# Weight transfers of 4 MB with 32 KB rows, in a ring of four buffers and a fifth beside it

## What is computed

```
x = _L0_conv_ref(x, style, 2, 13)       # 13x13 Gaussian means and deviations of x and style: (x-mean_x)/std_x*std_s+mean_s
x = _L1_conv_ref(x, weights of L1)      # attention over patches and windows, below
x = _L2_conv_ref(x, w1, b1, w2, b2)     # two 3x3 convolutions, relu between, + x
x = _L3_conv_ref(x, weights of L3)      # as L1, other weights

# L1 and L3: PD = 1024, WD = 16384, 4 windows (of 32x32), 16 patches (of 8x8) in each, 8 heads
fl = _ln(xf, pn_g, pn_b)                                     # 64 patches x 1024
pf = _merge(_attn(fl, Wqk_p) @ _heads(fl @ Wv_p) + _dwconv(...)) @ Wout_p
ww = _attn(_ln(pl, pln_g, pln_b), Wqk_w, WDH)                # 4 x 4 per head, from the pooled image
wv = _heads(_ln(xw, wn_g, wn_b) @ Wv_w)                      # 4 x 16384 @ 16384 x 1024
wf = _merge(nds @ wv + _dwconv(wv, ...)) @ Wout_w            # 4 x 1024 @ 1024 x 16384
out = diag_scaled * pf + wf + x
```

## Time and profile before

| | us |
|---|---|
| median of 3 runs | 762.57 |
| lowest, highest | 761.68, 762.76 |
| span of the profiled execution, first to last instruction | 760.3 |
| TensorE busy in it | 499.3 (66%) |
| VectorE busy | 92.3 (12%) |
| DMA queue 1, share of the 16 engines' time | 99.1% |
| bytes moved | 320.82 MB |

### The profile page before, as it was taken

How to read it: one execution, slowest core, us unless ns; L and a number is a source line. 1 busy time by engine, 2 the same in 40 slices (tenths; PEclk the granted TensorE clock), 3 DMA queues, 4 the chain that set the end, 5 groups by cost and what they waited for, 6 DMA issues and landing times.

```text
span 760.3 us, 7405 instructions
## 1 busy us (share of the span) xinstructions
PE 499.3 (66%) x3076; PEld 143.4 (19%) x3076; DVE 92.3 (12%) x254; ACT 38.0 (5%) x79; POOL 8.8 (1%) x19
## 2 busy tenths in 40 slices
PE   6599675556556656565677979565665576666565
PEld 5234210000002211121122433000000121111121
DVE  3754400000001000000006071000000100000000
ACT  2111100000000000000001010000000000000000
POOL 2100000000000000000001000000000000000000
PEclk9589898786878777878897989978677877768789
DMA  9999999999999999999999999999999999999996
GB/s 367 427 391 431 427 428 428 429 428 428 428 428 429 428 428 428 428 428 429 428 428 427 424 428 427 431 428 428 428 428 428 428 428 428 428 430 428 429 428 280
DMA packets 22856, 320.82 MB, mean 422 GB/s; under 512 B 2569, under 2 KB 2689, under 8 KB 3257
## 3 DMA queue, kind: packets, MB, share of 16 engines
q1 hardware_dynamic: 22464, 320.04, 99.1%
q10 hardware_dynamic: 377, 0.56, 0.2%
HBM read 320.10 MB, written 0.49 MB: 422 GB/s over the span
## 4 chain that ended last, share of the span: by engine, by line
DMA 72%; PE 20%; DVE 6%; issue 1%; ACT 1%; SPq 0%; DVEq 0%; ACTq 0%
DMA ring<-stream 71%; PE bank L341 4%; PE bank L452 3%; PE bank L429 3%; PE bank L407 2%; DVE conv_p L772 2%; PE bank L350 2%; PE bank L259 1%; DMA cst<-const 1%; PE bank L358 1%; PE bank L476 1%; PE bank L270 0%; DVE l_sq L644 0%; PE bank L312 0%; PE bank L474 0%
## 5 line engine op out<-in xcount | busy, mean ns | idle before, releaser
L452 PE MATMUL bank<-ring,wf_t 128*32 128x512 f32 x1024 | 169.3, 797 | 99.1 <-DMA ring<-stream 93.7
L429 PE MATMUL bank<-ring,stage 128*4 128x512 f32 x1024 | 162.3, 773 | 107.5 <-DMA ring<-stream 107.5
L452 PEld LDWEIGHTS bank<-ring,wf_t 128*32 128x32 f32 x1024 | 32.7, 131 | 215.3 <-DMA ring<-stream 147.8
L429 PEld LDWEIGHTS bank<-ring,stage 128*4 128x4 f32 x1024 | 24.7, 94 | 243.3 <-DMA ring<-stream 163.6
L259 PE MATMUL bank<-cst,area 128*128 128x128 f32 (+1 forms) x234 | 38.5, 318 | 15.3 <-ACT area L579 11.6
L259 PEld LDWEIGHTS bank<-cst,area 128*128 128x128 f32 (+1 forms) x234 | 32.9, 219 | 43.9 <-ACT area L579 33.8
L847 DVE TENSOR_TENSOR image<-bank,image 128x32 f32 (+1 forms) x30 | 5.1, 194 | 278.3 <-PE bank L259 278.3
L341 PE MATMUL bank<-ring,area 128*64 128x512 f32 x128 | 33.7, 692 | 1.7 <-DVE area L728 1.7
L821 DVE COPY wv_t<-bank 128x32 f32<-128x32 f32 x2 | 0.4, 192 | 275.4 <-PE bank L259 275.4
L579 ACT COPY area<-bank 128x512 f32<-128x512 f32 x15 | 8.8, 586 | 282.3 <-PE bank L452 282.3
L407 PE MATMUL bank<-ring,area 128*64 128x512 f32 x64 | 18.0, 727 | 0.0
(11 more groups left out here) (193 smaller groups left out, 196.4 us busy)
## 6 DMA issues: line engine op xcount, KB each, us to landing
ring<-stream SPq DMA_DIRECT2D x151, 2048.0 KB, 35.5
ring<-stream SPq DMA_DIRECT2D x2, 1024.0 KB, 35.8
l_in<-images SPq DMA_DIRECT2D x1, 512.0 KB, 4.4
cst<-const SPq DMA_DIRECT2D x1, 461.0 KB, 5.6
area<-window_gains ACTq DMA_DIRECT2D x1, 256.0 KB, 4.6
windows_last<-area SPq DMA_DIRECT2D x1, 256.0 KB, 2.0
out<-l_in ACTq DMA_DIRECT2D x2, 112.0 KB
area<-small ACTq DMA_DIRECT2D x1, 52.0 KB
```

Of the source, the lines that this page charges most:

```text
L429: m = mm(bank[0][32 * j:32 * j + 4, :], stage[:, k // 8, at:at + 4], w[:, j], start=False, stop=False)
L452: m = mm(bank[6 + g][32 * j:32 * j + 32, :], wf_t[:, h, :], w[:, j], start=(h == 0 and onto is None), stop=(h == GROUP - 1))
```

## The change

- Every transfer of weights is four slots (`QUARTER`), 128 rows of 32 KB, except the last four slots: the last eight go as 4, 2, 1 and 1 slots (`LAST_CUTS`).
- `ring` stays 128 KB of a partition, now four places of four slots. A fifth place, `extra`, 32 KB, holds the first and the sixth four-slot piece of each layer. The six pieces ("quarters") are Wqk_p, Wv_p, Wqk_w and Wout_p.
- Wv_w and Wout_w are laid out on the host in blocks of eight slots ("halves"), 128 rows of 64 KB. A transfer takes one half of each row: 32 KB out of every 64 KB. In `quarters` rows are 32 KB and stand one after another.
- The work areas of the first stage lie in the ring's last place, so that the fifth piece waits for `image_turned`; `out_rows` lies in `extra`.
- TensorE waits once for four slots where it waited once for two. SyncE's waits follow: a place is filled again when its four slots have been used. In the second layer the pieces 1 and 2 wait for the first half of the first layer's last turn, the pieces 3 and 4 for all of it, and piece 0 for nothing of its own.
- The semaphore per buffer becomes one per piece and place: `quarter_landed`, `part_landed`, `last_landed`. A parameter makes the memory set aside for descriptors that software writes smaller.

The matmuls, their operands' shapes and their order stay as they are, and so does the work of ScalarE, VectorE and GpSimd.

```
-        ring = sb("ring", P, RING, PAIR * SLOT)
+        ring = sb("ring", P, TURN * SLOT)
+        extra = sb("extra", P, QUARTER * SLOT)
...
+        front = ring[:, 3 * QUARTER * SLOT:]
+        l0_in = front[:, 0:C * IMG].rearrange("p (c x) -> p c x", c=C)
...
+        out_rows = extra[0:IMG, 0:2 * BANK]
...
+            at = None if j in (0, N_QUARTERS - 1) else (j - 1) * QUARTER * SLOT
+            return extra[:, :] if at is None else ring[:, at:at + QUARTER * SLOT]
...
-            for k in range(RING):
-                sp.dma_start(ring[:, k, :], stream[k]).then_inc(ring_landed[k], 16)
-            def slots_free(t, k):
-                sp.wait_ge(slots_used, t * (RING * PAIR) + ((k + 1) * PAIR - RING * PAIR))
-
-            with sp.Fori(1, N_BUFFERS // RING - 1) as t:
-                for k in range(RING):
-                    slots_free(t, k)
-                    sp.dma_start(ring[:, k, :], stream[t * RING + k]).then_inc(ring_landed[k], 16)
...
+            def load_quarter(L, j):
+                sp.dma_start(quarter_of(j), quarters[L * N_QUARTERS + j]).then_inc(quarter_landed[j], 16)
+
+            def load_part(L, t, c):
+                lo = c % 2 * QUARTER * SLOT
+                sp.dma_start(ring[:, c * QUARTER * SLOT:(c + 1) * QUARTER * SLOT],
+                             halves[t * 2 + (L * N_HALVES + c // 2)][:, lo:lo + QUARTER * SLOT]).then_inc(part_landed[c], 16)
+
+            for L in range(2):
+                load_quarter(L, 0)
+                for j in range(1, N_QUARTERS - 1):
+                    if L:
+                        sp.wait_ge(slots_used, used(L, -HALF if j < 3 else 0))
+                    elif j == N_QUARTERS - 2:
+                        sp.wait_ge(image_turned, 1)
+                    load_quarter(L, j)
+                sp.wait_ge(slots_used, used(L, QUARTER))
+                load_quarter(L, N_QUARTERS - 1)
+
+                for c in range(4):
+                    sp.wait_ge(slots_used, used(L, (c + 2) * QUARTER))
+                    load_part(L, 0, c)
+                with sp.Fori(1, 2 * TURNS - L) as t:
+                    for c in range(4):
+                        sp.wait_ge(slots_used, t * TURN + (used(L, S_VW) + (c + 1) * QUARTER - TURN))
+                        load_part(L, t, c)
...
+            for n, landed in enumerate(last_landed):
+                lo, hi = LAST_CUTS[n], LAST_CUTS[n + 1]
+                sp.wait_ge(slots_used, used(1, S_VW) + t * TURN - HALF + hi)
+                sp.dma_start(ring[:, (HALF + lo) * SLOT:(HALF + hi) * SLOT],
+                             halves[2 * N_HALVES - 1][:, lo * SLOT:hi * SLOT]).then_inc(landed, 16)
```

More of the change, by code:

```diff
@@ L102, in constants, with build @@
     return c
-def build(nc, images, const, window_gains, small, l2w, stream, out, windows_last):
+def build(nc, images, const, window_gains, small, l2w, quarters, halves, out, windows_last):
     with ExitStack() as ctx:
@@ new lines, in _ @@
+            t = 2 * TURNS - 1
+            for c in range(2):
+                sp.wait_ge(slots_used, used(1, S_VW) + t * TURN + (c + 1) * QUARTER - TURN)
+                load_part(1, t, c)
+            for n, landed in enumerate(last_landed):
[3 more added lines that the diff above has]
+                             halves[2 * N_HALVES - 1][:, lo * SLOT:hi * SLOT]).then_inc(landed, 16)
@@ L259, in turn, with quarter_there, part_there @@
                 return mm(dst, src, ident[0:rows, 0:rows], start=True, stop=True)
[L261 to L264, removed]
+            def quarter_there(L, s):
+                if s % QUARTER == 0:
+                    pe.wait_ge(quarter_landed[s // QUARTER], 16 * (L + 1))
+            def part_there(L, t, c):
+                pe.wait_ge(part_landed[c], t * 16 + 16 * (L * 2 * TURNS + 1))
             pe.wait_ge(const_landed, 16)
@@ L421, in _ @@
                 with pe.Fori(0, TURNS) as i:
[L422 to L423 removed]
+                    for k in range(TURN):
+                        if k % HALF == 0:
                             pe.wait_ge(staged, i * 2 + (2 * TURNS * L + k // 8 + 1))
[L425 to L426 removed]
+                        if k % QUARTER == 0:
+                            part_there(L, i, k // QUARTER)
+                        w = slot_of(S_VW + k).rearrange("p (j n) -> p j n", j=4)
                         for j in range(4):
@@ L445, in group @@
                     for h in range(GROUP):
[L446 to L450, removed]
+                        if onto is None and h % QUARTER == 0:
+                            part_there(L, i + TURNS, g * 2 + h // QUARTER)
+                        elif onto is not None and h in LAST_CUTS:
+                            pe.wait_ge(last_landed[LAST_CUTS.index(h)], 16)
+                        w = slot_of(S_OUTW + g * GROUP + h).rearrange("p (j n) -> p j n", j=4)
                         for j in range(4):
@@ L888, in dram @@
         return nc.dram_tensor(name, a.shape, mybir.dt.from_np(a.dtype), kind="ExternalInput").ap()
-    gains, smalls, pieces = [], [], []
+    gains, smalls, first, rest = [], [], [], []
     for n in ("L1_conv", "L3_conv"):
@@ L895 @@
         smalls += [v[k].reshape(P, 9).T for k in ("conv_p_w", "conv_w_w")]
-        pieces += [in_tiles(arr(f"{n}_{k}"), PAIR * SLOT // arr(f"{n}_{k}").shape[1]) for k in ("Wqk_p", "Wv_p", "Wqk_w", "Wout_p", "Wv_w")]
+        first += [in_tiles(arr(f"{n}_{k}"), QUARTER * SLOT // arr(f"{n}_{k}").shape[1]) for k in ("Wqk_p", "Wv_p", "Wqk_w", "Wout_p")]
+        rest += [in_tiles(arr(f"{n}_Wv_w"), HALF * SLOT // PD)]
         out_w = arr(f"{n}_Wout_w")
-        pieces += [in_tiles(out_w[:, at:at + SLOT], PAIR) for at in range(0, WD, SLOT)]
-    stream = dram("stream", np.concatenate(pieces))
+        rest += [in_tiles(out_w[:, at:at + SLOT], HALF) for at in range(0, WD, SLOT)]
+    quarters, halves = dram("quarters", np.concatenate(first)), dram("halves", np.concatenate(rest))
     l2w = np.concatenate([arr(f"L2_conv_{k}").transpose(1, 2, 3, 0).reshape(C, 9 * C) for k in ("w1", "w2")]
```

65 lines of the change are left out of this document (32 added, 33 removed).

## The result

| | kernel before | changed kernel |
|---|---|---|
| median, us | 762.18 (761.68 to 762.76, 4 runs) | 755.18 (754.87 to 755.32, 4 runs) |
| ratio | | 0.9906, 95% interval 0.9894 to 0.9918 |
| span of the profiled execution, us | 760.3 | 753.0 |
| packets | 22856 | 12056 |

The change makes the kernel 7.0 us faster, 0.94%. The forecast was 757.6 us with a range of 754.3 to 763.0: the sign and the range held. The forecast gain was 4.9 us and the measured one is 7.0; the rest of the 2.4 is that the kernel before has a median of 762.57 us ahead of the prediction and of 762.18 here. Two more comparisons of the same two kernels, on other chips, gave 0.9902 and 0.9907.

A forecast was written before the change was run, and what follows sets the result against it. The prediction took the DMA weight stream to bound the kernel. From a span of 760.3 us it took 3.7 for the rate and 1.2 for the dry moment, then added 2.27 between span and median: 757.6 us, range 754.3 to 763.0.

The forecast's parts named there:

- What bounds the kernel: Whole kernel: the DMA weight stream at 428 GB/s sets the time, with 72% of the chain waiting for weights.
- The rate: Weight stream: half as many packets, each with a fixed cost of 2 to 8 ns, saves 3.7 us including semaphores.
- Half as many transfers, half as many semaphores: Weight stream: fewer semaphore packets are within the rate's gain or add at most 0.7 us.
- The dry moment: First layer, near 45 us: with twenty slots queued the stream no longer runs dry, saving 1.2 us, bounds 0 and 1.7.
- the deduction for an engine that might catch up: Gap near 45 us: one late DMA engine may have used it, so 1.2 us was taken instead of 1.7.
- No other dry place: Steady turns, the first stage's softmax pause and the layer change: no gain and no loss.
- The tail: After the last landing: 4.3 us stay, a change of zero, with up to 2 us more if the clock falls.
- the rival of the tail: Longer TensorE bursts and pauses lower the clock, so the tail grows by 2 us: 759.6 us, chance 0.06.
- The forecast's own last step: Adding the 2.27 us between span and median to the 755.4 us span, giving 757.6 us.
- the cut rows: Weight stream: each 32 KB row becomes two 16 KB packets; 761.4 us, chance 0.13 shared with free packets.
- the free packets: Weight stream: a packet's fixed cost is nothing, so 428 GB/s stays; 761.4 us, chance 0.13 shared with cut rows.
- The layout: Wv_w and Wout_w in HBM: reading 32 KB out of every 64 KB is slower; 765 to 772 us, chance 0.11.

The follow-up runs named there:

- The versions with 8 MB blocks: Changed kernel with Wv_w and Wout_w in 8 MB transfers of 64 KB rows: 754.08 us; one transfer cut in two, 754.20; a second cut too, 755.07.
- the added wait: Changed kernel, but the first layer's fifth piece also waits for two used slots, so only 16 slots are queued when TensorE starts: 757.09 us, ratio 0.9932.
- the unbroken blocks: Changed kernel with each piece of Wv_w and Wout_w stored as one contiguous 4 MB block instead of 32 KB out of every 64 KB: 755.42 us, ratio 0.9917.

## Why the prediction was right, and where it was short

**What bounds the kernel:** right. The stream did before and does now, and nothing outside it moved the time.

**The rate:** the mechanism was right, one fixed cost for every packet, and the size was not. The term stood at 3.7 us; it is 5.6 (760.67 - 755.04), which is the prediction's upper bound. The step that failed is the reading of the cost at 2 to 8 ns from the packets' durations. It set a row of 8 KB from the very end, 312 ns, where seven rows moved while the other engines had nothing left to do, against rows of 16 KB from the full stream, 615.6 ns. In the full stream a row of 8 KB takes longer. The DMA view of 200 to 210 us (packets, MB, share), first of the kernel with rows of 8 KB, then of the changed kernel:

```profile
q1 hardware_dynamic: 532, 4.23, 101.4%
...
q1 hardware_dynamic: 153, 4.36, 101.2%
```

Without their 16 and 20 semaphore packets that is 314 ns for a row of 8 KB and 1217 ns for one of 32 KB. Durations from like stretches would have given 13 to 14 ns for a joint (2 x 314.4 - 615.6, and 2 x 615.6 - 1217.4), too much: the paces are 310.6, 611.9 and 1214.4 ns (39.76, 39.16 and 38.86 us over 128, 64 and 32), 3 to 4 ns under each duration, so packets that follow each other on an engine overlap by that much. The difference of the paces is 9.3 and 9.4 ns. The prediction had nearly the right number in its hands, in the sentence that took the whole distance to the 435 GB/s as a cost per packet and came to 6 us; it put that aside as over the bound.

**Half as many transfers, half as many semaphores:** up to 0.7 us was granted; the runs with 4 and 2 MB transfers show none. The prediction counted 74 transfers fewer and 1,184 semaphore packets; it is 75 and 1,200 (under 512 B the page counts 2569 before and 1369 after), which with the 9,600 makes the 10,800.

**The dry moment:** 1.2 us forecast, 1.7 measured, by two kernels, and up to 2.1 by the last landings of two traces. The bytes missing in the two windows, 0.71 MB or 1.7 us, were the right measure as they stood; the deduction for an engine that might catch up was not needed. That a part of the loss is slow first packets and not standstill, the prediction didn't see, though the share of 1.05 at 270 GB/s says it. That 20 queued slots would be enough, and that the sixth piece would go out before 52 us (48.42), held.

**No other dry place:** held for the changed kernel. The second layer starts on its weights 30.8 us after the last piece of the first (408.23 - 377.41), 28.7 before: the 2 us more that four slots in one go were said to cost, and hidden as said. The versions with 8 MB blocks show what that margin is worth: there it was used up, near 434 us and, with no cut, near 474.

**The tail:** 4.3 us before, 753.0 - 748.77 = 4.2 now. In an execution of the same kernel on another chip the last landing is at the same 748.77 us, but the last eight matmuls took 1.82 us instead of 1.07, at a granted clock of 0.56 instead of 1.00, and the run was 0.8 us longer (755.91 against 755.14). Timeline of that execution:

```profile
748.77 1.82 PE L487 MATMUL bank<-ring,wf_t 128*32 128x512 f32 x8 [1.40 <-DMA ring<-halves]
```

So the rival of the tail exists, as a scatter of under 1 us, and not as a loss of the change.

**The sum:** 5.6 + 1.7 = 7.3 us, against 7.0 to 7.2 measured. The 5.6 comes from the rows of 16 KB and the 1.7 from the added wait, two kernels that don't depend on each other. (The forecast's own last step, 755.4 + 2.27, rounds to 757.7, not 757.6.)

**The rivals:** the cut rows fall with the packet count, the free packets with the kernels of 16 and 8 KB rows. The layout falls with the unbroken blocks; the 10,800 packets and the 432 GB/s had pointed there already.

## What to carry to other kernels

When a kernel is bound by its DMA stream and the engines are busy all the time, count the packets: here each cost 9.4 to 10 ns of its engine from 8 KB to 64 KB, so 16 KB rows lose 1.5% and 32 KB rows 0.8%, and it was the length of the contiguous row that counted, not whether a transfer had 2 or 4 MB. Read such a cost from the pace, that is from the times at which two landings far apart release the waiting engine, and not from packet durations, least of all from stretches that are loaded unlike. Before transfers are made larger, work out for each stage start how much is queued and when the first place comes free: coarser places come free later, and 8 MB blocks turned a margin into new dry moments. Look for them in every stage of the trace: one was found and cut here while a neighbour nearly as large stayed.

## What the hardware showed that was not expected

- The cost per packet is the same, 9.4, 9.4 and 10 ns, at steps from 8 to 16, 16 to 32 and 32 to 64 KB, and extrapolated to none the stream would run at 435 GB/s.
- A row of 64 KB goes as one packet: 7592 packets in all, where the 32 KB rows make 12056.
- Rows 2 MiB apart in HBM cost 5.5 us of 755, in a few stretches alone; from 120 to 370 us the rate stayed at 432 GB/s. For rows 1 MiB apart no cost is shown.
- When a queue had just run out, the packets of the next transfer started about 1 us after its issue, and the first ones of 32 KB took 1.5 to 2.2 us instead of 1.22.
- Twice as many transfers (2 MB instead of 4 MB) cost nothing that can be measured: 760.56 against 760.67 us.
